# Three run-time tables of a graph kernel, stored as unsigned 16-bit numbers in place of signed 32-bit ones

## What is computed

```python
def _spmm(src, dst, w, x, n):
    return jax.ops.segment_sum(w[:, None] * x[src], dst, num_segments=n)
...
edge_index = jnp.stack([src, dst])
x = x + _L0_gnn_ref(_layernorm(x, axis=-1), src, dst, edge_weight, ...)
x = x + _L0_ffn_ref(_layernorm(x, axis=-1)[None], ...)[0]
x = x + _L1_gnn_ref(_layernorm(x, axis=-1), edge_index, ...)
x = x + _L1_ffn_ref(_layernorm(x, axis=-1)[None], ...)[0]
```

## Time and profile before

| | us |
|---|---|
| median of 3 runs | 1825.73 |
| lowest and highest | 1823.91, 1827.79 |
| span of the profiled execution | 1822.0 |
| set-up, up to the first matmul of the build | 46.9 |
| build, up to the last clear of accumulators by ACT | 46.9 to about 539 |

### The profile page before, as it was taken

One profiled execution on the slowest core, in us unless ns is written; L12 is line 12 of the kernel. 1 busy time (PEld: TensorE's weight loads), 2 busy tenths in 40 slices (PEclk: granted clock), 3 DMA queues, 4 the chain that ended last, 5 costly groups with the idle time before them and its releaser, 6 DMA issues.

```text
span 1822.0 us, 30852 instructions
## 1 busy us (share of the span) xinstructions
PE 1704.3 (94%) x10162; PEld 1363.7 (75%) x10163; DVE 942.9 (52%) x1593; ACT 569.8 (31%) x854; POOL 186.2 (10%) x260
## 2 busy tenths in 40 slices
PE   6999999888879999999999999999999999998995
PEld 4898988888766777777777777767677777787784
DVE  7999999998862300111144443552312243245436
ACT  2135677888880100000011111343400000004442
POOL 4000000000000100000000000000000000153683
PEclk9999999999999999999999999999999999999998
DMA  4203344544569445454443435900054434434375
GB/s 98 1 34 124 146 175 192 206 201 200 228 239 356 132 139 154 134 161 149 138 127 110 127 124 149 232 1 0 15 187 167 141 110 120 151 117 132 106 241 183
DMA packets 136919, 261.73 MB, mean 144 GB/s; under 512 B 22236, under 2 KB 74735, under 8 KB 136606
## 3 DMA queue, kind: packets, MB, share of 16 engines
q1 hardware_dynamic: 116824, 237.02, 40.2%
q0 software_dynamic: 5808, 14.70, 2.2%
q10 hardware_dynamic: 14230, 9.29, 1.7%
HBM read 161.13 MB, written 108.09 MB: 148 GB/s over the span
## 4 chain that ended last, share of the span: by engine, by line
issue 55%; PE 27%; ACT 6%; DVE 4%; ACTq 3%; DMA 2%; POOL 1%; DVEq 1%; SPq 0%; POOLq 0%
PE ps L2112 12%; PE ps L2113 4%; PE ps L2143 3%; ACT wide L870 3%; ACTq L914 2%; PE ps L2363 2%; ACT ps L818 2%; PE ps L2347 2%; DVE act_c L1373 1%; PE ps L2355 1%; PE ps L2339 1%; PE ps L2160 0%; ACTq L859 0%; DMA count_matrix<-wide 0%; PE ps L2015 0%
## 5 line engine op out<-in xcount | busy, mean ns | idle before, releaser
L2143 PE MATMUL ps<-wide 128*128 128x320 f32 (+1 forms) x2000 | 533.2, 427 | 0.0
L2143 PEld LDWEIGHTS ps<-wide 128*128 128x128 f32 x2000 | 378.4, 190 | 141.3 <-issue 0.4
L2112 PE MATMUL ps<-early,act_c 128*128 128x200 bf16 x2400 | 295.7, 252 | 43.4 <-issue 18.7
L2143 PE MATMUL ps<-wide,act_a 128*128 128x320 f32 (+1 forms) x1000 | 264.4, 426 | 2.3 <-DMA wide<-weight_matrix 2.2
L2112 PEld LDWEIGHTS ps<-early,act_c 128*128 128x128 bf16 x2400 | 220.5, 97 | 58.1 <-issue 57.3
L2143 PEld LDWEIGHTS ps<-wide,act_a 128*128 128x128 f32 x1000 | 189.8, 190 | 75.4 <-DMA wide<-weight_matrix 2.4
L870 ACT COPY wide<-ps 128x832 f32<-128x832 f32 x200 | 169.8, 849 | 121.8 <-PE ps L2113 120.6
L818 ACT ACTIVATE ps<-wide 128x832 f32 (+1 forms) x200 | 173.4, 868 | 42.0 <-ACT wide L870 33.7
L1373 DVE TENSOR_TENSOR act_c<-act_a,pair_tab 128x3072 bf16<-128x3072 bf16 x98 | 169.1, 1750 | 14.6 <-PE ps L2113 14.6
L1501 DVE TENSOR_TENSOR wide<-ps,rows 128x1280 f32<-128x1280 f32 x10 | 14.9, 1491 | 283.5 <-PE ps L2160 283.5
L2112 PE MATMUL ps<-act_a,act_c 128*128 128x200 bf16 x1152 | 140.3, 251 | 11.0 <-ACT ps L818 4.2
(11 more groups left out here) (261 smaller groups left out, 1808.5 us busy)
## 6 DMA issues: line engine op xcount, KB each, us to landing
wide<-weight_matrix SPq DMA_DIRECT2D x90, 800.0 KB, 4.5
wide<-count_matrix SPq DMA_DIRECT2D x45, 800.0 KB, 4.6
weight_matrix<-wide SPq DMA_DIRECT2D x60, 480.0 KB, 2.5
count_matrix<-wide SPq DMA_DIRECT2D x60, 480.0 KB, 2.6
weight_matrix<-wide SPq DMA_DIRECT2D x20, 560.0 KB, 2.7
count_matrix<-wide SPq DMA_DIRECT2D x20, 560.0 KB, 2.7
wide<-weight_matrix SPq DMA_DIRECT2D x20, 400.0 KB, 3.7
routed_tokens<-in_x_dram SPq DMA_DIRECT2D x2, 3072.0 KB, 30.4
```

Of the source, the lines that this page charges most:

```text
L2112: nc.tensor.matmul(weights, hot_parts[:, slot % PART_SLOTS, part, two, :, k], hot_key[mask_slot][:, mask_two, 0:WCOLS, k], start=False, st ...
L2143: i = nc.tensor.matmul(ps[:, 2 * sub + h, 0:n], features[:, q * QUADS + t, h * P:(h + 1) * P], moving, start=q == 0 and t == 0, stop=q == ...
```

## The change

The three tables hold unsigned 16-bit numbers. `line_tab` moves from `early` to the free end of `rows` (columns 1520 to 2259 of 2304); the int32 intermediate values stay in `early`, under the names `bank_i` and `free_i`. The last step of each table writes the 16-bit result to its new place: for the banks a multiplication by 512.0 in place of the shift, for the group numbers the same addition. `end_tab` stays where it is, and only its element becomes 16 bits wide. The number of instructions and their order on each engine are the same; the numbers of the program's lines rise by 4.

```diff
--- before.py
+++ after.py
@@ -18,6 +18,7 @@
 BF16 = mybir.dt.bfloat16
 I32 = mybir.dt.int32
 U32 = mybir.dt.uint32
+U16 = mybir.dt.uint16
 AX = mybir.AxisListType.X
 ds = bass.ds
 
@@ -353,6 +354,7 @@
         hot_lane = [masks(act_c_flat, PART_SLOTS * part_cols, mask_cols), masks(act_a_late, 0, mask_cols), masks(act_a_late, mask_cols, mask_cols)]
         own_row = act_a_late[:, 2 * mask_cols + key_cols:2 * mask_cols + key_cols + PARTS]
         rows_flat = rows[:, :, :].rearrange("p a b -> p (a b)")
+        line_cols = PPAD // LINE * LINE_COLS
         key_wide = rows_flat[:, 0:WCOLS].bitcast(BF16).rearrange("p (c k) -> p c k", k=2)
         at = WCOLS
         lane_wide = rows_flat[:, at:at + P].bitcast(BF16).rearrange("p (m k) -> p m k", k=2)
@@ -362,16 +364,18 @@
         pair_key = rows_flat[:, at:at + PPAD // 2].bitcast(BF16)
         at += PPAD // 2
         pair_dst = rows_flat[:, at:at + PPAD // 2].bitcast(BF16)
+        at += PPAD // 2
+        line_tab = rows_flat[0:1, at:at + line_cols // 2].bitcast(U16)
+        assert at + line_cols // 2 <= 9 * D
+        bank_tab, free_tab = (line_tab.rearrange("p (a q) -> p a q", q=LINE_COLS)[:, :, q] for q in (slice(0, LINE), slice(LINE, LINE_COLS)))
 
         reached = [early[:, j * PPAD // 2:(j + 1) * PPAD // 2].bitcast(BF16) for j in range(WGROUPS)]
         pair_iota = degree_row[:, PPAD:2 * PPAD]
         window_of, chunk_of = work[:, 1000:1000 + PPAD], degree_row[:, 0:PPAD]
 
-        line_cols = PPAD // LINE * LINE_COLS
-        line_tab = early[0:1, 0:line_cols].bitcast(I32)
-        line_rows = line_tab.rearrange("p (a q) -> p a q", q=LINE_COLS)
-        bank_tab, free_tab = line_rows[:, :, 0:LINE], line_rows[:, :, LINE:LINE_COLS]
-        end_tab = early[0:1, line_cols:line_cols + (BUNITS + 1) * ENDS].bitcast(I32)
+        line_rows = early[0:1, 0:line_cols].bitcast(I32).rearrange("p (a q) -> p a q", q=LINE_COLS)
+        bank_i, free_i = line_rows[:, :, 0:LINE], line_rows[:, :, LINE:LINE_COLS]
+        end_tab = early[0:1, line_cols:line_cols + (BUNITS + 1) * ENDS // 2].bitcast(U16)
         end_rows = end_tab.rearrange("p (u e) -> p u e", u=BUNITS + 1)[:, :, 0:UGROUPS]
         disorder_tab = early[0:1, line_cols + (BUNITS + 1) * ENDS:line_cols + (BUNITS + 1) * ENDS + 1].bitcast(I32)
         hot_key_at = line_cols + (BUNITS + 1) * ENDS + 4
@@ -1295,18 +1299,18 @@
             dve.tensor_reduce(chunk_min[:, 0:CROWS], d3, AX, ALU.min).then_inc(chunk_ends, 1)
 
             dve.wait_ge(windows_taken, 1)
-            dve.tensor_copy(bank_tab, window_of[0:1, :].rearrange("p (a q) -> p a q", q=LINE)).then_inc(dve_chain, 1)
-            dve.tensor_copy(free_tab, window_of[0:1, :].rearrange("p (a b q) -> p a b q", q=QUAD, b=LINE_QUADS)[:, :, :, QUAD - 1]).then_inc(dve_chain, 1)
+            dve.tensor_copy(bank_i, window_of[0:1, :].rearrange("p (a q) -> p a q", q=LINE)).then_inc(dve_chain, 1)
+            dve.tensor_copy(free_i, window_of[0:1, :].rearrange("p (a b q) -> p a b q", q=QUAD, b=LINE_QUADS)[:, :, :, QUAD - 1]).then_inc(dve_chain, 1)
             dve.wait_ge(dve_chain, count(2))
-            dve.tensor_single_scalar(bank_tab, bank_tab, ACCS - 1, op=ALU.bitwise_and).then_inc(dve_chain, 1)
+            dve.tensor_single_scalar(bank_i, bank_i, ACCS - 1, op=ALU.bitwise_and).then_inc(dve_chain, 1)
             dve.wait_ge(next_min, 1)
             dve.tensor_tensor(unsorted, chunk_max, next_ps, ALU.is_gt).then_inc(chunk_ends, 1)
-            dve.tensor_single_scalar(free_tab, free_tab, 1, op=ALU.logical_shift_right).then_inc(dve_chain, 1)
+            dve.tensor_single_scalar(free_i, free_i, 1, op=ALU.logical_shift_right).then_inc(dve_chain, 1)
             dve.wait_ge(dve_chain, count(2))
-            dve.tensor_single_scalar(bank_tab, bank_tab, 9, op=ALU.logical_shift_left).then_inc(dve_chain, 1)
+            dve.tensor_scalar_mul(bank_tab, bank_i, 512.0).then_inc(dve_chain, 1)
             dve.wait_ge(gathered, 3)
             dve.scalar_tensor_tensor(pair_dst, window_of, -32.0 * WIN, over_banks(0), ALU.mult, ALU.add).then_inc(gathered_taken, 1)
-            dve.tensor_scalar_add(free_tab, free_tab, 1.0).then_inc(dve_chain, 1)
+            dve.tensor_scalar_add(free_tab, free_i, 1.0).then_inc(dve_chain, 1)
             dve.wait_ge(pair_windows, 2)
             starts = ps[0:1, 7, 0:WINDOWS].rearrange("p (g b) -> p g b", b=GROUP)[:, :, 0]
             first_half = slice(HALF + 1, HALF + 1 + (BUNITS - 1) * UGROUPS)
```

## The result

| kernel | median, us | lowest to highest | span of the profiled execution |
|---|---|---|---|
| before | 1826.76 (4 runs) | 1823.91 to 1832.52 | 1822.0 |
| with the change | 2249.77 (4 runs) | 2248.9 to 2250.5 | 2247.1 |

The change makes the kernel slower by 23%: the ratio is 1.2301 with a 95% interval of 1.2262 to 1.2340. The forecast was 1826.0 with a range of 1819 to 1834.

What follows compares the result with a forecast made beforehand. DVE was taken to set the build's pace from 120 to 298 us, no engine to be full until 400, ACT to set the end. Terms summed to 0 on the 1822.0 us span; median 3.7 above, so 1826.0, range 1819 to 1834.

Steps and rivals of the forecast that it cites:

- the first of the change's parts: PE's 74 line-table loads of 20 numbers: price goes by the number, count unchanged, so change 0; chance 0.73.
- The step's far end: PE's loads: most a 16-bit number might cost extra, 0.04 us each, from the quiet-to-loaded gap.
- a 16-bit access costs more: PE's and ACT's register loads: dearer half-words; 10 ns a number gives 8.6 us, 1834; decides from 4 ns; chance 0.15.
- its own sensitivity: Each extra ns a number: 20 ns on 16 lines, half of 14, and 16 earlier; 10 ns on 8 ACT loads.
- The faster rival: PE's and ACT's loads cost by bytes: about 13 us gained, 1813; chance 0.10, another 0.02 for a partial gain.
- The DVE steps: Last set-up steps on DVE: multiplication 0.77 us, addition 0.30; term 0, with ends of 0 and +1.2 us.
- The doubled rate: DVE's set-up steps with 16-bit output: doubled rate keeps the sum at 0; single rate would add 0.4 us.
- Place and address: Line table moved to `rows`, same partition, same single address instruction ahead of the load: cost 0.
- The end table on DVE: Its four set-up instructions keep shape, order and place, on far fewer numbers, under the same cover: 0.
- ACT sets the end of the build: End of the build, 500 to 540 us: ACT's instructions fill 37.08 of 40 us, so the end is ACT's.

Runs made afterwards that it cites:

- the run on low halves: Kernel before, int32 line table in its old place, waits masked; PE reads only each number's low half as uint16 with step 2: 2271.46 against 1858.06 us.
- The cuts into four: PE's line load split into four loads of 5: on the kernel before with int32 tables and masked waits, 2114.81 us; on the 16-bit change, 2137.76 us.
- The two aligned loads: Kernel before with int32 tables and masked waits; PE's line load split into 12 and 8 numbers, both from 16-byte boundaries: ratio 1.0154 to the kernel before.

## Why the prediction was wrong, point by point

**The step that failed** is the first of the change's parts: "I take the price by the number: change 0". The price does not go by the number; it goes by the access, and an access holds four numbers only if they are 32-bit, in a row and from a 16-byte boundary. The step's far end, 40 ns a number more, was also too low by four times: 236 - 68 = 168 ns.

The rows contained the hint. The slope on PE was 0.064 us a number, on ACT 0.155. I took the second for the first under load. But PE's load under DMA traffic was there too: 2.135 us for 20 numbers, 0.103 each with the fixed 0.076 taken off, still far from 0.155. By accesses the two come close: PE's 20 numbers are five, (2.135 - 0.08) / 5 = 0.41 us each, ACT's 10 are four (two of four numbers and two single ones), (1.572 - 0.08) / 4 = 0.37. And "64 ns each" was a mean over groups of four, 0.25 us per group, read as if it were the thing itself.

The Trainium skill (Runtime: NRT & Kernel Launch, Instruction fetch mechanics) gives a price of about 200 ns for each register, on a page that speaks of loads from HBM, where these tables lie in SBUF. The prediction set it aside since it differed from 64 ns. It is near the 236 ns of a single access measured here, and an estimate by it puts the quiet load after the change at 4.0 us, where 4.72 was measured; the load before, 1.36, is far from it.

**The rival that came true** is the second, "a 16-bit access costs more", with its place and its sign right, and its point of decision (4 ns a number) passed forty times over. Its reason was wrong: int32 numbers with a step cost the same 4.73 us, so it isn't the cutting out of a half-word, and half-words on 4-byte boundaries cost the same 4.72 (the run on low halves). Its price was too low even for the right number: 168 ns by its own sensitivity, 860 ns of time for each ns, gives 144 us, where 423 were lost. Two terms are missing in it. It counted 39 of the 74 lines (16, 7 and 16), as if DVE's pace or ACT's held in the others; with 3.4 us more a line PE's loads set the path in all 74, which by itself is 74 x 3.36 = 249 us, 284 under DMA. And it had no term for the clock: PE's 153.0 us of longer matmuls. The cuts into four show it at 0.99 to 1.00 with gaps of 1 us, at about the same busy share of PE.

**The faster rival** (bytes) is excluded by every run that reads 16 bits: half the bytes never made a load shorter.

**What was right.** The DVE steps: 0.77 and 0.30 us and a term of 0. The doubled rate held with a 16-bit output, as the Trainium skill (VectorE: DVE Perf Modes, What auto-detection actually checks) has it: 0.77 us with either output. Place and address: no cost from lying in `rows` (4.72 us there, and in `early` in the run on low halves). The end table on DVE: 0. The set-up's L1340 starts 0.01 us earlier.

**What no longer holds** is that ACT sets the end of the build: its copies (L874) idle 527 us for PE, where they idled 121.

**What stays open.** The two aligned loads cost 16 us against one because PE is late 0.6 us a line behind them in place of 0.34, and the lead is shown to shrink; what takes the lead away, the start of a load or the masks beside it, I didn't separate. Why the clock falls in one pattern of gaps and not in the other: their length, the work in between and its rate all differ. And what disturbs the loads at 40 to 46 us.

## What to carry to other kernels

Tables that a sequencer reads into registers belong in 32-bit numbers, in a row, from a 16-byte boundary, in multiples of four: one access of 0.25 us then brings four, and in every other form (16 or 8 bits, a step, another start) it brings one. Padding shortens the load: 12 numbers for 10 took 1.05 us in place of 1.57. If a value has to be bounded, a mask on the register (32 ns, some 0.6% of this kernel) is far cheaper than a narrow type (23%), and before a price "per number" is used for a new form, look whether the rows it comes from share a form.

## What the runs showed of the hardware that I had not expected

- A register load of 20 int32 takes 1.36 us or 4.73 us by nothing but its start or its step; loads of five int32, at every 20 bytes, made one kernel 14% slower, some 57 us of the 245 by the cut and the rest by the starts.
- The granted clock was 0.79 with gaps of about 4 us ahead of each line's 64 matmuls, and 1.00 with gaps of about 1 us ahead of each quad's 16, while PE was busy for 66% and 65% of the window. After a long gap the same matmul lasts 0.38 us, against 0.25 us ahead of it.
- A sequencer that needs 0.244 us a pair against PE's 0.36 hides a load of 1.36 us entirely in two lines of three if it comes once in 16 pairs, and doesn't hide one of 0.33 us once in 4 (PE's next matmul comes some 0.2 us late). What it hides by is the lead it has built, and small operations eat that lead.
